# First attention layer's loads and stores reordered, loads eight batches ahead, unit keys' parts made in its loop

## The reference

```python
# layers 0 and 2 (layer 2 without unit keys), for each of 16 sequences b:
xn = layernorm(x)                               # 64 tokens x 256
q, k = eight "heads" of 8 rows x 256 columns of xn and of the context
s = q.T @ k / sqrt(8)                           # 256 x 256 a head
out = softmax(s) @ v                            # v from the context
x = x + out                                     # layer 2: x + gamma * out
# layer 1: the same with keys of unit length over all heads' rows
# and a factor 5 in place of 1/sqrt(8)
# feed-forward of layer 0: two products with weights rounded to -1, 0, 1
# and activations rounded to eight bits, GELU twice between them
```

## Time and profile before

| | |
|---|---|
| median of three runs | 1334.82 us (1333.0 to 1335.53) |
| the profiled execution's own time | 1329.65 us |
| its span, first to last instruction | 1327.8 us |
| TensorE products busy | 1086.0 us, 82% |
| VectorE, ScalarE, POOL busy | 672.9, 636.7, 535.4 us |
| moved by DMA | 132.42 MB |
| granted TensorE clock, mean | 0.898 |

### The profile page before, as it was taken

One profiled execution on the slowest core, in us unless ns is written; L12 is line 12 of the kernel. 1 busy time (PEld: TensorE's weight loads), 2 busy tenths in 40 slices (PEclk: granted clock), 3 DMA queues, 4 the chain that ended last, 5 costly groups with the idle time before them and its releaser, 6 DMA issues. The chain is left out here.

```text
span 1327.8 us, 19221 instructions
## 1 busy us (share of the span) xinstructions
PE 1086.0 (82%) x6655; PEld 778.3 (59%) x6656; DVE 672.9 (51%) x1377; ACT 636.7 (48%) x1007; POOL 535.4 (40%) x592
## 2 busy tenths in 40 slices
PE   2988714489599994999489999999867569999997
PEld 0445401344288871555378888888634357888886
DVE  5667588741453336787643333333568653333333
ACT  4556537579544434677333344444374334344332
POOL 5132243001236652122256666666310316666663
PEclk9989855789879995899689999999988778999999
DMA  5655121168314314342133343333000013333331
GB/s 172 206 153 161 51 83 28 40 144 224 99 57 123 111 43 132 105 135 77 50 99 111 111 164 121 114 118 114 21 8 1 2 56 125 114 118 114 112 115 55
DMA packets 65796, 132.42 MB, mean 100 GB/s; under 512 B 9291, under 2 KB 33035, under 8 KB 65094
## 3 DMA queue, kind: packets, MB, share of 16 engines
q1 hardware_dynamic: 62326, 124.15, 31.5%
q10 hardware_dynamic: 3408, 7.47, 1.7%
HBM read 115.55 MB, written 15.45 MB: 99 GB/s over the span
## 5 line engine op out<-in xcount | busy, mean ns | idle before, releaser
L1404 POOL TENSOR_TENSOR f_hid<-f_gated,f_coef 128x512 f32<-128x512 f32 x152 | 224.0, 1475 | 161.6 <-DVE f_gated L1435 150.2
L1435 DVE TENSOR_TENSOR f_gated<-f_act_g,f_p_u 128x512 f32<-128x512 f32 x152 | 104.5, 688 | 261.9 <-PE f_p_u L1267 258.1
L796 ACT ACTIVATE a_probs<-a_p_sc 128x1024 f32<-128x1024 f32 x192 | 189.1, 1020 | 31.7 <-PE a_p_sc L710 24.1
L1344 ACT ACTIVATE f_hid_hi<-f_hid 128x512 fp32r<-128x512 f32 x152 | 96.1, 632 | 206.4 <-POOL f_hid L1404 206.3
L925 DVE TENSOR_REDUCE a_maxes<-a_p_max 128x2 f32<-128x512 f32 x256 | 160.0, 680 | 55.0 <-PE a_p_max L677 54.7
L1439 DVE TENSOR_TENSOR f_hid_lo<-f_hid,f_hid_hi 128x512 fp32r<-128x512 f32 x152 | 105.6, 695 | 151.3 <-ACT f_hid_hi L1344 150.9
L1339 ACT ACTIVATE f_act_g<-f_p_g 128x512 f32<-128x512 f32 x152 | 90.8, 597 | 160.8 <-PE f_p_g L1267 160.7
L677 PE MATMUL a_p_max<-a_k,a_q 72*128 72x256 bf16 x512 | 98.9, 318 | 50.4 <-DMA a_q<-q_parts 40.4
L710 PE MATMUL a_p_sc<-a_q,a_k 75*128 75x256 bf16 (+1 forms) x768 | 121.0, 287 | 10.5 <-ACT a_probs L796 4.7
L1280 PE MATMUL f_p_y<-f_hid_hi,f_down_hi 128*128 128x512 f32 x304 | 119.5, 393 | 7.0 <-issue 7.0
L1391 POOL TENSOR_TENSOR f_up_lo<-f_w,f_up_hi 128x512 fp32r<-128x512 f32 x76 | 98.0, 1290 | 56.7 <-ACT f_up_hi L1329 56.7
(11 more groups left out here) (283 smaller groups left out, 1682.8 us busy)
## 6 DMA issues: line engine op xcount, KB each, us to landing
f_w<-in_w SPq DMA_DIRECT2D x76, 384.0 KB, 3.5
f_coef<-coef SPq DMA_DIRECT2D x51, 512.0 KB, 3.7
a_q<-q_parts SPq DMA_DIRECT2D x48, 288.0 KB
a_k<-k_plain SPq DMA_DIRECT2D x96, 96.0 KB
outs<-a_out SPq DMA_DIRECT2D x48, 128.0 KB, 1.7
a_whole<-outs SPq DMA_DIRECT2D x48, 128.0 KB, 2.6
q_parts<-a_q_part SPq DMA_DIRECT2D x48, 96.0 KB, 3.2
a_k<-k_unit SPq DMA_DIRECT2D x24, 192.0 KB
```

The costliest lines, as they stand in the source:

```text
L796: nc.scalar.activation(probs[b % 2][:, 2 * pair:2 * pair + 2, :, :].rearrange("p h t d -> p h (t d)"), p_sc[pair % 2][:], ACT.Exp, scale=s ...
L1344: nc.scalar.activation(hid_hi[slot(t, 2)][c][:], hid[c][:], ACT.Copy).then_inc(hid_hi_done, 1)
L1404: nc.gpsimd.tensor_tensor(hid[c][:], gated[c][:], coef[slot(t, 2)][:, c * 512:(c + 1) * 512], ALU.mult).then_inc(hid_done, 1)
L1435: nc.vector.tensor_tensor(gated[c][:], act_g[c][:], p_u[c][:], ALU.mult).then_inc(gated_done, 1)
```

## The change

The large loads of layer 0 are issued by ScalarE once the context's first tile is there, one before and one after its first copy. SP stores all groups of keys (layer 0) and queries and asks for eight batches ahead of the loop, in layers 0 and 2; in the loop, batch b + 7 is asked for behind the store of output b - 1 and ahead of the read-back of output b - 3. The unit keys are loaded in the opening of layer 0 behind the first values, squared two batches of POOL earlier, clamped after maximum 68, rooted by ScalarE after batch 6, inverted by VectorE after maximum 76, and cut into parts by POOL in its batches 8 to 15, one chunk in each, once the plain keys' parts that lay in the same memory are stored. In the ternary stage the 24 stores stay, without waits for parts.

```diff
@@ -339,9 +339,6 @@
     def load(self, act, a):
         act.dma_start(self.keys[:], a["ctx_heads"]).then_inc(self.loaded, 16)
 
-    def ready(self, sp, part, c):
-        sp.wait_ge((self.hi_ready, self.mid_ready, self.lo_ready)[part], c + 1)
-
     def add_square(self, pool, c):
 
         tt, src = self.nc.gpsimd.tensor_tensor, self.keys[:, c, :]
@@ -393,7 +390,6 @@
 
     for c in range(CH):
         for part in range(3):
-            m.unit_keys.ready(sp, part, c)
             dst = bass.AP(m.k_unit.tensor, m.k_unit.offset + (3 * c + part) * HEADS * D,
                           [[3 * CH * HEADS * D, B], [D, HEADS], [1, D]])
             sp.dma_start(dst, m.unit_part[:, part, c, :]).then_inc(stored, 16)
@@ -592,15 +588,29 @@
                     load_q(1)
                     load_k(1)
                     store_k(1)
+                    store_k(2)
+                    load_k(2)
                     store_q(1, 0)
                     store_q(1, 1)
-                    load_k(2)
+                    load_k(3)
                     load_q(2)
                     load_q(3)
-                    load_k(3)
-                    store_k(2)
+                    store_k(3)
                     store_q(2, 0)
                     store_q(2, 1)
+                    load_k(4)
+                    store_k(4)
+                    load_q(4)
+                    store_q(3, 0)
+                    store_q(3, 1)
+                    load_k(5)
+                    load_q(5)
+                    load_k(6)
+                    load_q(6)
+                    store_q(4, 0)
+                    store_q(4, 1)
+                    load_k(7)
+                    load_q(7)
                 elif layer == 2:
                     load_k(0)
                     load_ones()
@@ -647,16 +669,11 @@
                                 load_q(b + 4)
                             if b % 2 == 0:
                                 load_unit_pair(b // 2 + 2)
-                    elif b + 4 < B:
-                        load_k(b + 4)
-                        load_q(b + 4)
                     if b >= 1:
                         store_out(b - 1)
-                    if with_max and b in (0, 1):
-                        if layer == 0:
-                            store_k(b + 3)
-                        store_q(b + 3, 0)
-                        store_q(b + 3, 1)
+                    if with_max and b >= 1 and b + 7 < B:
+                        load_k(b + 7)
+                        load_q(b + 7)
                     if b >= 3:
                         load_whole(b - 3)
                 for b in (B - 3, B - 2):
@@ -804,10 +821,10 @@
                     nc.scalar.activation(out[b % OUTS][:], p_out[:, 0:D], ACT.Copy).then_inc(out_copied, 1)
 
                 if layer == 0:
+                    act.wait_ge(keys_loaded[0], 16)
                     act.dma_start(m.x[:, 1:NI, :], a["x"][:, 1:NI, :]).then_inc(m.x_loaded[1], 16)
+                    key_parts.high(0)
                     act.dma_start(keys[:, 1:NI, :], a["ctx"][:, 1:NI, :]).then_inc(keys_loaded[1], 16)
-                    act.wait_ge(keys_loaded[0], 16)
-                    key_parts.high(0)
                     norm.scalar(act, 0)
                     key_parts.mid(act, 0)
                     act.wait_ge(norm.xn_ready, 1)
@@ -834,6 +851,7 @@
                     norm.apply_by_act(4)
                     norm.apply_by_act(5)
                     load_v(0)
+                    unit_keys.load(act, a)
                     parts.mid(act, 2)
                     act.wait_ge(norm.xn_by_act, 4)
                     parts.high(3)
@@ -903,8 +921,8 @@
                             load_neg(b + 2)
                         if layer == 0 and b in (1, 5, 9):
                             load_v(b // 4 + 1)
-                        if layer == 0 and b == 1:
-                            unit_keys.load(act, a)
+                        if layer == 0 and b == 6:
+                            unit_keys.root(act)
                     else:
                         exps(b, 2)
                         if b >= 1:
@@ -1001,8 +1019,10 @@
                                 dve.sem_inc(ident_ready, 1)
                         take_max(n)
                         if layer == 0:
-                            if n == 10 * HEADS + 4:
+                            if n == 8 * HEADS + 4:
                                 unit_keys.clamp(dve)
+                            if n == 9 * HEADS + 4:
+                                unit_keys.invert(dve)
                         i, at = divmod(n - 61, 16)
                         if 0 <= i < 4 and at % 4 == 0:
                             invert(i, 16 * at, 64)
@@ -1078,14 +1098,17 @@
                             add_tile(b // 2 - 4)
                         if b + 2 < B:
                             split_max(b + 2)
-                        if layer == 0 and 4 <= b < 8:
-                            for c in range(2 * (b - 4), 2 * (b - 3)):
+                        if layer == 0 and 2 <= b < 6:
+                            for c in range(2 * (b - 2), 2 * (b - 1)):
                                 unit_keys.add_square(pool, c)
+                        if layer == 0 and b >= B - CH:
+                            if b == B - CH:
+                                for g, (lo, hi) in enumerate(CUTS):
+                                    pool.wait_ge(k_stored[g], 16 * (hi - lo))
+                            for what in range(5):
+                                unit_keys.split(pool, one, what, b - (B - CH))
                     for i in range(4, LATE):
                         add_tile(i)
-                if layer == 0:
-                    for g, (lo, hi) in enumerate(CUTS):
-                        pool.wait_ge(k_stored[g], 16 * (hi - lo))
                 pool.wait_ge(added, LATE)
 
 
@@ -1689,11 +1712,6 @@
                 @block.gpsimd
                 def _(pool):
                     nc.gpsimd.memset(ones[:], 1.0).then_inc(ones_set, 1)
-                    pool.wait_ge(ones_set, 1)
-                    for c in range(CH):
-                        for what in range(5):
-                            m.unit_keys.split(pool, ones, what, c)
-
                 @block.tensor
                 def _(pe):
                     pe.wait_ge(ones_set, 1)
@@ -1719,7 +1737,6 @@
                 @block.scalar
                 def _(act):
                     norm.scalar(act)
-                    m.unit_keys.root(act)
                     for n in range(2):
                         act.wait_ge(loaded[n], 16)
                         if n == 1:
@@ -1764,7 +1781,6 @@
                     link = Link(dve, chain)
                     norm.vector(dve, link)
                     link(v.tensor_reduce(largest[:], m.xn[:], axis=AX.X, op=ALU.max, apply_absolute_value=True))
-                    m.unit_keys.invert(dve)
 
                     dve.wait_ge(meaned, 1)
                     link(v.tensor_scalar(w_mean[:], p_mean[:, 0:2], 1.0 / (D * INNER), 1e-5, ALU.mult, ALU.max))
```

## The result

The changed kernel takes 1348.15 us (median of 4 runs, 1347.02 to 1353.0) against 1334.01 (4 runs) for the kernel before beside it: a ratio of 1.0114, interval 1.009 to 1.0137, 14.1 us slower where 4.8 were forecast. The profiled execution took 1347.35 us with a span of 1345.6, against 1329.65 and 1327.8.

| stage | before, us | after, us | difference |
|---|---|---|---|
| attention, layer 0 | 169.8 | 173.8 | +4.0 |
| ternary stage | 84.4 | 76.5 | -7.9 |
| attention, layer 1 | 104.4 | 107.6 | +3.2 |
| its feed-forward | 141.8 | 137.6 | -4.2 |
| attention, layer 2 | 141.9 | 162.1 | +20.2 |

What follows compares the result with a forecast made beforehand. In both attention loops TensorE was taken as nearly full, with what ends its rare gaps setting the time. 0 - 8.2 - 4.7 + 13 + 8.2 + 1 + 1.5 - 6 = +4.8 us gave 1339.6, range 1324 to 1353.

Steps and rivals of the forecast that it cites:

- POOL's splits: Layer 0's loop: late splits of maxima and memory shared with VectorE cost +1.5 us (0 to +4).
- rival D: Layer 0, batch 6: its loads still arrive late and the main stall stays; +8.2 us, 1348; chance 0.05.
- The order: Loops of layers 0 and 2: loads ahead of the read-back make VectorE wait, 6.5 us a layer; +13 (+10 to +23).
- The clock after those waits: Layers 0 and 2: low TensorE clock behind late read-backs, 1.9 us each, five of six counted; +8.2 (-1.3 to +20).
- Loads eight ahead: Layer 0, batch 6: the 4.36 us stall goes, and 10.3 us of low clock worth 3.8; -8.2 us.
- The late read-back at 130.60: Layer 0 past iteration 8: emptier queue removes 2.2 us of idle and 2.5 of low clock; -4.7 (0 to -4.7).
- Unit keys in the loop: Layer 0: root on ScalarE and inversion on VectorE fall just ahead of the wait at maximum 77; +1 (0 to +4.3).
- The ternary stage: Between layers 0 and 1: splits and inversion leave, VectorE's tile instructions shorten; -6 us, between 2.9 and 11 saved.
- The opening: Start of layer 0: 3 us gain on the first tile against up to 5 lost; taken as 0 (-3 to +5).
- Rival C: Layer 0, batch 0: first scores late, 12 KB of maxima queued behind 2 MB; 4.5 us more, 1344; chance 0.18.
- A: TensorE's clock holds through the short read-back waits; 9.5 us fall away, 1330.1; chance 0.20.
- B: Layers 0 and 2: the read-back isn't late, so the 13 us go as well; 1317; chance 0.12.

Runs made afterwards that it cites:

- the read-back first: The changed kernel with the read-back of an older output issued straight behind the store again, ahead of the two loads, in layers 0 and 2: 1319.7 us, ratio 0.9893.
- the version with waits of 1.8 to 2.7 us: The kernel before with only layer 2's order changed: loads of the batch four ahead stand between store and read-back; 1344.67 us, ratio 1.014.
- the other trace: Trace of the changed kernel with the unit keys' load, squares, root, inversion and splits put back where they were before: 1355.77 us, ratio 1.0165.
- the values in pieces: The kernel before with the values of batches 4 to 15 asked for in twelve pieces of 256 KB instead of three of 1 MB: 1320.9 us, ratio 0.9923.
- the version with the root in the gap: The kernel before with the unit keys moved, their root ahead of an output copy where ScalarE waits, the inversion in four pieces: 1315.2 us, ratio 0.989.

## Why the prediction was right and wrong

The sign, the mechanism and its places were right: three late read-backs in layer 2, in front of the inversions after maxima 61, 77 and 93, with a low clock behind each; the ternary stage shorter; no stall at batch 6. The size was short by 9 us. Layer 2 grew by 20.2 us where 6 to 15 were forecast, and layer 0 had two such waits, not three. By the prediction, a longer layer 0 without the stall was to speak for POOL's splits; its 4.0 us more were the order's, since with the read-back first layer 0 took 162.1. The time is also that of rival D, 1348, whose stall isn't there: the number alone would have named the wrong cause. The two halves of the sum can be held against one run, the read-back first. All but the order came to 0 - 8.2 - 4.7 + 1 + 1.5 - 6 = -16.4 in the forecast and to -14.3 there (1319.7 against 1333.99). The order and the clock behind it came to +21.2 and to +28.5. So the second half was mis-sized. That the first came out near its forecast is partly luck: within it the loads eight ahead were forecast at -12.9 and alone are worth 4.1, and the unit keys with their stage were forecast at -3.5 and alone are worth 16.1.

- **The order, +13.** Shown as a mechanism, undersized: VectorE's waits sum to 9.15 us in layer 2 and to 6.35 in layer 0 (3.78, 0.28, 2.29), 15.5 in all. The mis-sized term is the 0.5 us for the landing. At the three inversions of layer 2 the landings were 4.0, 4.1 and 3.5 us, 0.9 to 1.5 more than before; that leaves 1.9, 1.9 and 1.5 us for the later issue, where 1.9, 1.5 and 1.5 were forecast. In layer 0 the unit keys' work took the place of the second wait. The Trainium skill, "DMA: Bandwidth & Descriptors", section on queues, rings and completion order, has the rule that was on the table: descriptors are consumed in ring order on each engine. The runs agree that the landing grows behind a load (2.4 to 2.7 us without, 3.3 to 5.3 with); I had chosen the value near the quiet end.
- **The clock after those waits, +8.2.** Undersized, and by these traces the larger share of the miss. In layer 2 23.9 us at the low clock cost 8.8, not 3 x 1.9 = 5.7. Layer 0 had 27.3 us of it against 13.7 with the read-back first: 5.0. Together 13.8 against 9.5 before its deduction of 1.3. I had priced each wait by the short low pieces of rows 1 and 4, whose idle was 2.2 us; here TensorE idled up to 3.0. How firm the 8.8 is stays open: the same code had 17 us of low clock, 6.3, in the other trace. In the version with waits of 1.8 to 2.7 us the old price held within 1.3 us.
- **Loads eight ahead, -8.2.** The stall went, but the gain was put down to the wrong part. The prediction named the unit keys' 1 MB beside the late asking for batch 6 and gave the whole 8.2 to the asking; the 1 MB, which the change also moved, was booked only as a risk to the opening. Two runs show that moving it is enough. It is worth 6.5 us alone (0.9951), the loads eight ahead 4.1 alone (0.9969) with the stall left on the maxima's rows.
- **The late read-back at 130.60, -4.7.** Right in kind. It stood at the fourth inversion, and none of the five traces with the loads eight ahead and 1 MB of values has a wait there, the changed kernel's included; all six with the loads four ahead have one, of 0.74 to 2.52 us. So the 2.52 it was priced by was the longest of six, and -4.7 is likely too much. With the values in pieces it goes as well, without any change in SP's queue.
- **Unit keys in the loop, +1.** Right, as far as one trace each can say. 2.0 us of idle and 10.2 us of low clock (3.8) follow the root, 5.8 in all. But both pieces of work fell under VectorE's wait at maximum 77, as said: it was 0.28 us with them and 2.89 without, where TensorE's idle and low clock cost 4.9. The difference is 0.9. Where no read-back is late, the root has its own price: 1.7 us of idle in both versions, with 10.2 us of low clock behind it with the read-back first and 3.4 with the keys alone moved. Each table load took 1.28 us and the root started 0.02 behind it (99.16 + 1.28 to 100.46), so the drain of 1.38 us that the Trainium skill adds ("ScalarE: Activation LUTs", section on what a table load costs) isn't seen here either. By the times it is small: the place of the 1 MB (-6.5) and the ternary stage (-7.9) make -14.4, and with root, inversion and splits in the loop the measured sum was -16.1 (0.9879), within its interval.
- **POOL's splits, +1.5.** Behind the first turn, TensorE waits over 0.5 us for POOL in the changed kernel's two loops only where VectorE or ScalarE was late just before. Nearer to 0.
- **The ternary stage, -6.** -7.9; tile instructions of 0.344 us as said.
- **The opening, 0.** Right: +1.0 us at the turn of the second batch (46.95 against 45.92), and no difference by itself. Rival C was wrong: with 2 MB ahead of them, the first maxima's rows were there at 35.40 us, not after 37.2. Its 4.5 us weren't worked out either; 40 - 37.2 is 2.8.
- **Rivals A, B and D** fell: the clock didn't hold, layer 2 wasn't as long as before, the stall didn't stay.
- **Not in the sum:** +3.2 and -4.2 us in layer 1 and its feed-forward, +2.8 in the last two stages, and the two low pieces at the end of layer 2. The first pair stands in most versions, at +2.9 to +3.6 and -2.1 to -4.2, also where only layer 0's transfers were moved. The low pieces come in some versions and not in others, behind idles of 0.65 and 0.77 us that the kernel before has too. Their cause stays open.

## What to carry to other kernels

In one queue put the small transfer that somebody waits for ahead of the large one nobody needs yet; it pays for what stands ahead twice, in issue time (2.9 us here) and in landing (0.9 to 1.5). When a transfer looks late, look at what else was in flight in its own queue and in the others before moving it ahead: in layer 0 of the kernel before the keys, the maxima's rows and the read-back were late in turn, and each time the wait went when 1 MB asked for in the loop was moved or cut. And a bundle is tested part by part: one part of this one was worth 16 us alone, another cost 28.

## What the runs showed of the hardware that I had not expected

- The landing of a 128 KB read-back grew behind a load in its own queue: 2.4 to 2.7 us behind nothing, 3.4 to 4.4 behind 288 KB, 3.3 to 5.3 behind 576 KB.
- 12 KB behind 2 MB in one queue took up to 11.3 us, and the other queue suffered too: a read-back that SP issued meanwhile, at 66.56, landed 9.6 us later (in the version with only the loads eight ahead).
- The price of an idle isn't its length alone, and it varies between executions. Single idles of 0.94 us had nothing behind them in one trace and 3.4 us of low clock in another; of 1.04 to 1.06 us at the root, 3.4 us in two traces and nothing in a third; 1.7 us in three pieces at the root, 3.4 in one trace and 10.2 in another. Two pieces at a late read-back, 1.5 to 2.2 us together, had 3.4 to 10.2 us behind them, and 2.3 to 3.0 us together 6.8 to 10.2.
- A copy on ScalarE ran behind a square root without a table load between them (in the version with the root in the gap, 85.65 and 85.97; the load comes only with the next exponential):

```profile
84.35 1.28 ACT L362 ACT_TABLE_LOAD   x1
85.65 0.42 ACT L362 ACTIVATE early_ulength<-early_ulength 128x256 f32<-128x256 f32 x1
85.97 0.37 ACT L801 ACTIVATE a_out<-a_p_out 128x256 f32<-128x256 f32 x1
86.35 1.28 ACT L793 ACT_TABLE_LOAD   x1
```
